# A recommendation tower on one core: gathered tables in new banks, the last MLP by tile, high parts in PSUM

## What is computed

```
e = jnp.stack([tbl_0[ids[:, 0]], ..., tbl_25[ids[:, 25]]], axis=1)
combined = jnp.concatenate([dense_features[:, None, :], sparse_features], axis=1)
interactions = jnp.einsum('bnd,bmd->bnm', combined, combined)
interactions_flat = interactions[:, _TRIU_I, _TRIU_J]
z = jnp.concatenate([dense_features, interactions_flat], axis=1)
h = jnp.concatenate([z, r_dense_features], axis=1)
h = jnp.maximum(h @ W_top1 + b_top1, 0.0)
h = jnp.maximum(h @ W_top2 + b_top2, 0.0)
y = h @ W_top3
```

## Time and profile before

| | us |
|---|---|
| median of 3 runs | 384.8 (383.59 to 385.23) |
| the profiled execution | 385.81 |
| its span, first to last instruction | 383.9 |
| PE busy | 333.5 (87%) |
| POOL busy | 269.4 (70%) |
| VectorE busy | 260.9 (68%) |
| ACT busy | 169.3 (44%) |

### The profile page before, as it was taken

One profiled execution on the slowest core, in us unless ns is written; L12 is line 12 of the kernel. 1 busy time (PEld: TensorE's weight loads), 2 busy tenths in 40 slices (PEclk: granted clock), 3 DMA queues, 4 the chain that ended last, 5 costly groups with the idle time before them and its releaser, 6 DMA issues.

```text
span 383.9 us, 13545 instructions
## 1 busy us (share of the span) xinstructions
PE 333.5 (87%) x6208; PEld 303.5 (79%) x6208; DVE 260.9 (68%) x206; ACT 169.3 (44%) x248; POOL 269.4 (70%) x277
## 2 busy tenths in 40 slices
PE   3777895949899998999899989999898989969787
PEld 2656784939898897979898879889897889859676
DVE  3999889574849865787668775777666776723322
ACT  2553563514445443545364543544354434532412
POOL 6787777777777777777777777777777777776000
PEclk9999998797999999999999999999999999997999
DMA  7996124251224322242215221341224112332020
GB/s 181 234 236 188 51 70 112 57 158 50 56 55 118 88 58 56 66 144 52 56 51 158 51 57 54 94 121 50 56 66 143 51 50 58 97 99 56 2 92 0
DMA packets 18985, 33.51 MB, mean 87 GB/s; under 512 B 5834, under 2 KB 11666, under 8 KB 18930
## 3 DMA queue, kind: packets, MB, share of 16 engines
q0 software_dynamic: 8848, 18.11, 18.2%
q1 hardware_dynamic: 10082, 14.55, 13.5%
HBM read 28.96 MB, written 3.68 MB: 85 GB/s over the span
## 4 chain that ended last, share of the span: by engine, by line
PE 40%; POOL 34%; issue 13%; DVE 7%; DMA 3%; ACT 2%; DVEq 0%; SPq 0%
POOL rows L390 34%; PE gram_ps L714 8%; PE hot_ps L684 8%; PE mlp_ps L684 8%; PE mlp_ps L720 4%; DVE one_hot L538 3%; PE transpose_ps L650 3%; PE mlp_ps L721 3%; PE mlp_ps L722 3%; DVE units L527 2%; DMA rows<-table,ids_sb 1%; PE hot_ids_ps L659 1%; PE mlp_ps L761 1%; DMA rows<-bounce 1%; DVE packed_lo L549 1%
## 5 line engine op out<-in xcount | busy, mean ns | idle before, releaser
L390 POOL DMA_INDIRECT rows<-table,ids_sb x272 | 268.5, 987 | 83.5 <-issue 80.7
L538 DVE TENSOR_TENSOR one_hot<-hot_ids_ps,row_numbers_sb 125x2048 fp32r<-125x2048 f32 x72 | 165.2, 2298 | 72.2 <-PE hot_ids_ps L659 62.7
L684 PE MATMUL hot_ps<-one_hot,table_hi 125*128 125x256 f32 x320 | 82.5, 295 | 3.4 <-issue 2.9
L684 PE MATMUL hot_ps<-one_hot,table_lo 125*128 125x256 f32 x320 | 79.6, 286 | 0.0
L684 PE MATMUL mlp_ps<-one_hot,table_hi 125*128 125x256 f32 x256 | 66.6, 297 | 11.8 <-DVE hidden_lo L569 6.4
L684 PEld LDWEIGHTS hot_ps<-one_hot,table_hi 125*128 125x128 f32 x320 | 62.1, 194 | 4.6 <-issue 4.6
L714 PE MATMUL gram_ps<-embed_t 128*27 128x27 f32 x4096 | 54.9, 195 | 11.2 <-issue 4.8
L684 PE MATMUL mlp_ps<-one_hot,table_lo 125*128 125x256 f32 x256 | 63.8, 286 | 0.0
L714 PEld LDWEIGHTS gram_ps<-embed_t 128*27 128x27 f32 x4096 | 45.0, 106 | 23.0 <-issue 15.4
L684 PEld LDWEIGHTS hot_ps<-one_hot,table_lo 125*128 125x128 f32 x320 | 62.3, 195 | 0.1
L684 PEld LDWEIGHTS mlp_ps<-one_hot,table_hi 125*128 125x128 f32 x256 | 49.9, 195 | 14.6 <-DVE one_hot L538 7.4
(11 more groups left out here) (80 smaller groups left out, 381.4 us busy)
## 6 DMA issues: line engine op xcount, KB each, us to landing
rows<-table,ids_sb POOLq DMA_INDIRECT x272
embed_t<-table SPq DMA_DIRECT2D x8, 448.0 KB
bounce<-units SPq DMA_DIRECT2D x8, 448.0 KB, 2.6
scratch<-bounce SPq DMA_DIRECT2D x7, 378.0 KB
dense_sb<-dense_t SPq DMA_DIRECT2D x8, 128.0 KB
scratch<-w SPq DMA_DIRECT2D x1, 512.0 KB, 4.8
units<-w_units SPq DMA_DIRECT2D x2, 252.0 KB
scratch<-table SPq DMA_DIRECT2D x1, 448.0 KB
```

The lines of the kernel that those rows point to most:

```text
L390: nc.gpsimd.indirect_dma_start(rows[:, t2, f - 1, :], None, tables[table], bass.IndirectOffsetOnAxis(ids_sb[:, tile, table:table + 1], 0)) ...
L538: nc.vector.tensor_tensor(one_hot[:, k % RING], ids.to_broadcast([HOT_P, HOT_STEPS, GROUP]), row_numbers_sb[:, :, None].to_broadcast([HOT_ ...
L684: last = nc.tensor.matmul(hot_bank(n), table[:, n, step, :], one_hot[:, k % RING, step, :], start=(step == 0 and table is table_hi), stop= ...
```

## The change

It changes seven things.

1. The 17 gathered tables are transposed in banks of 4, 3, 4, 4, 2.
2. For tile 15 the first two gathered tables are not fetched by POOL. SyncE loads their row numbers into registers, 16 at a time, and issues one DMA of 512 bytes for each of 256 rows into `last_rows`, behind its other work of groups 0 to 5.
3. The last MLP is done by tile. `units` of group 7 are packed in two halves (`pack_half`); the first tile's MLP (steps U0, A0 to A6; `first_half`) runs behind the second tile's gram in `hot_ps` and `hot_ids_ps`, the second tile's in `last_mlp`. All these products have 128 columns where those before had 256. There are 12 idle products in place of 36.
4. In the opening PE multiplies each `table_hi` by the identity into the two banks of `gram_ps` (`place_hi`), and VectorE subtracts from there.
5. ACT casts a hot table one table earlier.
6. M1 stands ahead of H2, and M5 ahead of H6. In the last group S0 comes first, then G0 and G1, and M5 stands at the end of its first tile.
7. `hot_ids` is loaded for 64 partitions, the rest zeroed by VectorE; `y` is kept in unused places of other tiles.

The diff, cut to what matters:

```diff
+SP_TABLES = 2
+SP_LOAD = 16
+SP_LOADS = [3, 3, 3, 3, 2, 2]
...
-TILE_BANKS = -(-GATHERED // PER_BANK)
+BANK_SIZES = [4, 3, 4, 4, 2]
+TILE_BANKS = len(BANK_SIZES)
...
-    "G0 S0 Q0 H0 M0 Q1 Q2 H1 G1 W0 Q3 H2 W1 M1 Q4 M2 W2 H3 W3".split(),
-    "G0 M3 Q0 H4 W4 M4 D0 E0 Q1 Q2 H5 W5 G1 Q3 H6 M5 Q4 H7 H8 M6".split(),
+    "G0 S0 Q0 H0 M0 Q1 Q2 H1 G1 W0 Q3 M1 H2 W1 Q4 M2 W2 H3 W3".split(),
+    "G0 M3 Q0 H4 W4 M4 D0 E0 Q1 Q2 H5 W5 G1 Q3 M5 H6 Q4 H7 H8 M6".split(),
...
-    "G0 S0 Q0 M0 Q1 G1 M1 M2 Q2 M3 D0 Q3 M4 Q4".split(),
-    "G0 M5 G1 M6".split(),
+    "S0 G0 G1 Q0 M0 Q1 M1 M2 Q2 M3 D0 Q3 M4 Q4 M5".split(),
+    "G0 U0 G1 M6 A0 A1 A2 A3 A4 A5 A6".split(),
...
-WARM_PRODUCTS = 36
+WARM_PRODUCTS = 12
...
+        def fetched_by_sp(tile, f):
+
+            return tile == TILE_COUNT - 1 and f <= SP_TABLES
...
+        def in_banks(table):
+
+            return table.rearrange("p (a j) d -> p a (j d)", a=2)
...
+        def half_bank(m):
+
+            return (hot_ps, hot_ids_ps)[m % 2][:, 0:P]
...
+            def pack_half(h):
+
+                place = bounce.rearrange("p x -> (p x)")[h * P * HALF_UNITS:(h + 1) * P * HALF_UNITS].rearrange("(p x) -> p x", x=HALF_UNITS)
+                sp.wait_ge(early_copied, ROUNDS * (GROUPS - 1) + TILE_ROUNDS * (h + 1))
+                sp.dma_start(place, last_units[:, h]).then_inc(units_stored, 16)
+                sp.wait_ge(units_stored, 16 * (GROUPS + h))
+                by_row = place.rearrange("(s n) x -> s (n x)", s=BLOCK)[:, 0:N * HALF_UNITS]
+                sp.dma_start(last_packed_raw[h].rearrange("p s c q -> p s (c q)"),
+                             by_row.rearrange("s (p x) -> p s x", p=UNIT_P)).then_inc(units_packed, 16)
...
+            def fetch_rows(loads):
+
+                for _ in range(loads):
+                    n, at = divmod(fetched["rows"], P)
+                    table = GATHERED_TABLES[n]
+                    with ExitStack() as held:
+                        numbers = [held.enter_context(sp.register(f"row{n}_{at + i}")) for i in range(SP_LOAD)]
+                        sp.load(numbers, last_ids[n:n + 1, at:at + SP_LOAD])
+                        for i, number in enumerate(numbers):
+                            row = sp.snap(number, min_val=0, max_val=ROWS[table] - 1)
+                            sp.dma_start(last_rows[at + i:at + i + 1, n, :], tables[table][bass.ds(row, 1), :]).then_inc(rows_fetched, 16)
+                    fetched["rows"] += SP_LOAD
...
+                if g < len(SP_LOADS):
+                    fetch_rows(SP_LOADS[g])
+
+            sp.wait_ge(units_packed, 16 * (GROUPS - 1))
+            pack_half(0)
             store_y(GROUPS - 2)
-            sp.wait_ge(units_packed, 16 * (GROUPS - 1))
-            pack(GROUPS - 1, 1, last_packed_raw)
+            pack_half(1)
+
+            sp.wait_ge(half_copied, MLP_USES)
             store_y(GROUPS - 1)
...
+                        if fetched_by_sp(tile, f):
+                            continue
...
             split_hi(0)
+            split_hi(1)
             for step, n in [(x[0], int(x[1:])) for x in FIRST_STEPS]:
                 if step == "H":
-                    if n + 1 < HOT:
-                        split_hi(n + 1)
+                    if n + 2 < HOT:
+                        split_hi(n + 2)
...
             def split_lo(k):
-                dve.wait_ge(hi_split, k + 1)
-                lower(raw_tables[k], table_hi[:, k], table_lo[:, k]).then_inc(lo_split, 1)
+                dve.wait_ge(hi_placed, k + 1)
+                nc.vector.tensor_tensor(in_banks(table_lo[:, k]), in_banks(raw_tables[k]), gram_ps[0:HOT_P, :, :],
+                                        ALU.subtract).then_inc(lo_split, 1)
...
+            def place_hi(k):
+                pe.wait_ge(hi_split, k + 1)
+                if k >= 1:
+                    pe.wait_ge(lo_split, k)
+                for a in range(2):
+                    last = nc.tensor.matmul(gram_ps[:, a, :], identity_r[0:HOT_P, :], in_banks(table_hi[:, k])[:, a, :],
+                                            start=True, stop=True)
+                last.then_inc(hi_placed, 1)
 
             def look_up(g, n):
...
+            def first_half(m):
+                out = half_bank(m)
+                g, columns = GROUPS - 1, half_columns(0)
+                if m >= 2:
+                    pe.wait_ge(half_copied, m if m == MLP_USES - 1 else m - 1)
+                if 2 <= m < H1_CHUNKS + 2:
+                    pe.wait_ge(half_split, min(m, H1_CHUNKS) if m >= H1_CHUNKS else m - 1)
+                if m < H1_CHUNKS:
+                    h = slice(m * P, (m + 1) * P)
+                    if m == 0:
+                        pe.wait_ge(dense_split_lo, g + 1)
+                        pe.wait_ge(units_lo, g + 1)
+                    three_products(out, (w1d_hi[:, h], w1d_lo[:, h]), (dense_half(dense_hi, 0), dense_half(dense_lo, 0)), True, False)
+                    for c in range(CHUNKS):
+                        last = three_products(out, (w1u_hi[0:unit_p(c), c, h], w1u_lo[0:unit_p(c), c, h]),
+                                              (packed_half(packed_hi, 0)[0:unit_p(c), :, c, :], packed_half(packed_lo, 0)[0:unit_p(c), :, c, :]),
+                                              False, c == CHUNKS - 1)
+                elif m < H1_CHUNKS + H2_CHUNKS:
+                    h = slice((m - H1_CHUNKS) * P, (m - H1_CHUNKS + 1) * P)
+                    for c in range(H1_CHUNKS):
+                        last = three_products(out, (w2_hi[:, c, h], w2_lo[:, c, h]),
+                                              (hidden1_hi[:, c, columns], hidden1_lo[:, c, columns]), c == 0, c == H1_CHUNKS - 1)
+                else:
+                    for c in range(H2_CHUNKS):
+                        last = nc.tensor.matmul(out[0:1, :], w3_sb[:, c:c + 1], hidden2[c][:, columns],
+                                                start=(c == 0), stop=(c == H2_CHUNKS - 1))
+                last.then_inc(half_ready, 1)
             def last_mlp():
...
             broadcast_ids(0)
+            place_hi(0)
...
                 if step == "H":
+                    if n + 1 < HOT:
+                        place_hi(n + 1)
                     look_up(0, n)
```

## The result

The changed kernel takes 397.5 us (median; 397.2 to 398.3) beside 385.0 for the one before in the same session: ratio 1.033, 95% interval 1.030 to 1.037. It is **slower**; the forecast was 379.2, its range 371.5 to 384.5. The profiled run has a span of 395.6.

A forecast was written before the change was run, and what follows sets the result against it. Neither PE (40% of the last chain) nor POOL (34%) was taken as the bound alone. Earlier gathers, the last group and the MLP by tile gave span 378.3 against 383.9: 384.8 - 5.6 = 379.2 us, range 371.5 to 384.5.

The forecast's parts named there:

- POOL: Gathers: table_lo from PSUM saves 5.0 us, two gathers fewer in the last tile 2.5; POOL ends at 346.4.
- rival 4: Reads from PSUM hold up POOL as before, tile 14 comes 5 us later: 384.2 us; chance 0.04.
- SyncE: Row fetching in groups' free time: 31 us of work in 38.6 us, hidden up to 0.55 us a row.
- rival 3: SyncE late: at 0.75 us a row, 6 to 12 us stay, 385 to 391; chance 0.05.
- The opening: VectorE's chain 2.5 us later, covered by POOL's earlier rows; PE reaches tile 4 near 104 instead of 109.95.
- The moved stages: M1 and M5 ahead of lookups: PE 40.3 us a group instead of 41.8, POOL 43.3; nothing at the end.
- The last group: Tiles 14 and 15 on PE: last Q4 at 349.0, G1 ends at 355.0, M6 at 355.9.
- Q4(t14) at 330.5: Tile 14's last transposes: fourth bank landed at 326.7, then Q3, M5, H6 (0.5 + 1.4 + 1.9).
- a hole of 0.8 again: PE's hole expected in the last tile's grams, G0 from 350.6 to G1's end at 355.0.
- The product: A product of 128 columns in the last MLP takes 0.11 us; bounds 0.059 and 0.213.
- rival 5: A hole in the last tile and half clock for 6.8 us: up to 3.4 us, 382.6; chance 0.10.
- rival 2: Products of 128 columns take 0.213 us: 14.8 us more, 394 us, slower than before; chance 0.08.

The follow-up runs named there:

- experiment 6: SyncE's fetching removed, POOL gathers all 272: on e11's kernel 379.1 us beside 375.6; on e6's kernel 551.2 beside 553.5.
- Experiments 4 and 5: e9's kernel with M2 to M6 of the group before moved, 16 idle products: 377.0 us; then also a stage between any two grams: 375.6 us.
- e2: The kernel before with nothing but the last MLP by tile: 391.6 us, ratio 1.014.
- e1: The changed kernel with the last MLP over all 256 rows at once again: 383.2 us, ratio 0.995.
- e3: The changed kernel with each product of A0 to A5 over 256 columns, the same 128 taken twice: 388.0 us, ratio 1.007.
- e10: e9's kernel with Q3, Q4 behind M1, M2 ahead of G0, M3 to M6 in the wait for packed units, 16 idle products: 377.0 us, ratio 0.979.
- e11: e10's kernel with a stage between any two grams: 375.6 us, ratio 0.974, the fastest kernel of the study.
- e9: e1's kernel with SyncE storing the last group's units before y of the group before: 383.1 us, ratio 0.993.
- e12: e11's kernel without SyncE's fetching, POOL gathering all 272: 379.1 us beside 375.6.
- e17: Second run of e16's kernel: 560.8 us, where the whole MLP in the same order and session took 549.3 to 549.4.
- e16: The changed kernel, MLP by tile, in e11's order, y stored behind both halves of the units: 565.4 us in a session near 550 us.
- e4: The changed kernel with 24 idle products of 256 columns in front of A0: 394.2 us, ratio 1.012.
- e6: The same program as e10, in a session near 550 us: 553.5 us beside 549.7 for the kernel before.

## Why the prediction was wrong, step by step

- **POOL: right.** Tile 14 from 306.4 (306.38), last gather 346.4 (346.8), no long gather beside a table_lo subtraction (rival 4 is out).
- **SyncE: right.** A row took 0.42 us from start to start (nine in 3.55), and the packs of the middle groups went out right behind the early copies (157.11 behind 157.08), so the fetching was hidden (rival 3 is out). It is worth 3.5 us once PE follows at POOL's heels, part of them by luck, as experiment 6 has it.
- **The opening: right.** PE was to reach tile 4 near 104 and did so at 103.39.
- **The moved stages: size wrong, no harm seen.** I had PE at 40.3 us a group; tiles 4 to 6 took 41.4 (103.39 to 144.82), where the earlier trace rows have 41.8. The waits of the earlier trace rows are gone, but 0.4 came of them, not 1.5.
- **The last group: 6.3 us late.** "Q4(t14) at 330.5" was 333.2: PE waited 1.40 for the rows of the bank before, which let it start 1.1 later than forecast, and then had half clock for 3.4 us (some 1.5 lost). Q4 of the last tile came at 352.3 (forecast 349.0). G1's hole was 1.77 where "a hole of 0.8 again" stood, but each gram ran in 1.27 instead of 1.82, so that the two took 4.3 us, as forecast (4.4). What counts is the hole of 2.19 in front of M6, where I had none, and M6 at half clock. Experiments 4 and 5 tie the holes to long runs of short products: G0, G1 and M6 in a row. The change puts them there, and the sum read their size off a kernel where M5 stood between.
- **The product: right.** 0.111 us against 0.11, and 0.118 for twice the columns. So at 128 columns it is not the columns that set it, which leaves the weight load, as the working from the earlier trace rows had it.
- **The clock is the step that failed.** The forecast took all 144 products at 0.11, the full clock's price, and left half clock to rival 5, "up to 3.4 us". That priced it by the one stretch of the earlier trace rows, 6.8 us among wide products, and carried its length over to a stage that has none. Here it lasted 27.3 us and cost 72 x 0.102 = 7.3 us in A0 to A5, 2.6 in the 24 products behind them, and some 1 in M6; with the 1.5 in the last group that is some 12 of the 17.3 us missed. Rival 5 took 382.6 us for what came to 397.5. What the clock does in a stage of other products has to be a case of its own.
- **And a sum that was never drawn.** My forecast has 23.3 us from the end of G1 (355.0) to that of the span (378.3), and the kernel before 19.5. The MLP by tile was thus 3.8 us *slower* in my own numbers, as run e2 at full clock confirms with 23.8 us (4.3 slower). It hid behind the gains ahead of it, which run e1 shows as a kernel of 383.2 with the old MLP. Half the rows cost PE as much as all of them, since 72 products of 0.11 us are added and none gets shorter. An edit has to be priced against leaving it out.
- The range failed with it: rival 2 gave 394 us and had 0.08, for a price of the product; nothing stood for the same price by the clock.

The expectations of the runs came out closer: e1, e3, e10 and e11 within 1% of their numbers, though e1 and e3 lie some 1 us outside the ranges given. Storing the units first was to bring 3.1 us and brought less than 1 (e9), SyncE's fetching was to bring 1.5 to 2.5 and brought 3.5 (e12), and the first half in the new order was to cost some 8 and cost 11.5 and 16 (e17, e16).

## What to carry to other kernels

Before splitting a stage to overlap it, ask what sets the time of one instruction: where the weight load does, half the columns take as long, and the split doubles the work. Price each edit of a bundle against the same kernel without it, by the time from a fixed point to the end, and look for real work to put into a wait before idle products. Carry a stretch of half clock over to another stage only if the same instructions run there. And where POOL gathers, look at what VectorE subtracts meanwhile: an operand read from PSUM instead of SBUF can shorten the gathers.

## What the runs showed of the hardware

- A stream of weight loads and products takes 0.111 us a product at 128 columns and 0.118 at 256 with the clock at 2.4 GHz, and 0.213 at both widths at 1.2 GHz. The Trainium skill (TensorE: Matmul & The Clock Gate, LDWEIGHTS) has columns / 1.2 ns for a load, 107 ns for 128, close to the 0.111 at full clock; its 81 ns for a stream of 128-column pairs (Back-to-back issue gap) no row of these fp32r products reaches.
- At half clock, products of 128 columns ran for 20.8 us (362.3 to 383.1) without the full clock coming back, while PE was busy for 24.2 of the 27.3 us; with 256 columns in their place half clock ended after 6.8 us. At full clock they kept it in runs e2 and e4 (profiled) and lost it in e16 and e17. The Trainium skill (TensorE: Matmul & The Clock Gate, HAM oscillation) ties the fall to waits in which PE stands idle; in run e17 it fell with no gap above 0.85 us in the 12 us before, so such waits alone do not account for it.
- VectorE's subtraction of two SBUF operands lengthens a gather that POOL issues meanwhile, by up to 0.99 us; with one operand in PSUM it does not. The Trainium skill (SBUF — State Buffer, Who interferes with whom) has such an instruction contend with GpSimd's reads of SBUF, and a gather reads its row numbers, `ids_sb`, there: the traces agree. It also infers that the writing of descriptors is not held up; which part of a gather gets longer no run here shows.
- PE's holes in runs of short instructions can grow, with the same program on another chip, from 3.9 us to 112.1 (runs e10 and e6).
